# Reordering VectorE's routing work in a fused attention and mixture-of-experts kernel

## The reference: what is computed

```
A   = softmax(Q K^T / 4)
out = (0.6 * A + 0.4 * L) V          # L: a band of three neighbours on each side
x   = x + out Wo^T + bo
```

```
xn     = layernorm(x)
probs  = softmax(gelu(xn rW1 + rb1) rW2 + rb2)          # router, 512 hidden features
mask   = the two largest of four;  gate = probs * mask
x      = x + sum_e gate_e * (gelu((xn*mask_e) We1[e] + be1[e]) We2[e] + be2[e])   # 1024 hidden
```

## Time and profile before

| what | value |
|---|---|
| median of three runs | 2059.73 us (2054.78 to 2060.18) |
| profiled execution, its own time | 2075.05 us |
| its span | 2073.3 us |
| TensorE busy in the span | 2006.5 us (97%) |
| VectorE busy | 1647.4 us (79%) |
| ScalarE busy | 1403.4 us (68%) |
| GpSimd busy | 393.8 us (19%) |
| mean granted TensorE clock | 0.988 |
| attention and projection stages | about 0 to 1437 us of the span |
| routing | about 1437 to 1605 us |
| experts | from about 1605 us to the end |

### The profile page before, as it was taken

How to read it: one execution, slowest core, us unless ns; L and a number is a source line. 1 busy time by engine, 2 the same in 40 slices (tenths; PEclk the granted TensorE clock), 3 DMA queues, 4 the chain that set the end, 5 groups by cost and what they waited for, 6 DMA issues and landing times. The chain is left out here.

```text
span 2073.3 us, 48468 instructions
## 1 busy us (share of the span) xinstructions
PE 2006.5 (97%) x16588; PEld 1077.1 (52%) x16588; DVE 1647.4 (79%) x2007; ACT 1403.4 (68%) x2502; POOL 393.8 (19%) x461
## 2 busy tenths in 40 slices
PE   7999999999999999999999999998998899999997
PEld 4543333333333333333333333334876799999996
DVE  6788999999999999999999999970445555665564
ACT  3348888888888888888888888887554322222221
POOL 1360010010001000100100010010054433333333
PEclk9999999999999999999999999999999999999998
DMA  7934354335334533543453355320125567776671
GB/s 264 242 78 90 74 119 93 71 87 120 79 72 99 115 72 74 121 91 71 87 120 79 72 105 109 71 61 25 57 100 219 213 236 267 260 255 237 244 261 52
DMA packets 102092, 267.69 MB, mean 129 GB/s; under 512 B 22894, under 2 KB 45936, under 8 KB 95344
## 3 DMA queue, kind: packets, MB, share of 16 engines
q1 hardware_dynamic: 91648, 241.25, 44.0%
q0 software_dynamic: 10368, 25.45, 3.5%
HBM read 212.87 MB, written 74.20 MB: 138 GB/s over the span
## 5 line engine op out<-in xcount | busy, mean ns | idle before, releaser
L588 DVE TENSOR_REDUCE part_max<-psum_attend 128x1 f32<-128x1024 f32 x1024 | 1241.9, 1222 | 59.4 <-PE psum_attend L710 47.1
L643 ACT ACTIVATE probs<-psum_attend 128x512 f32<-128x512 f32 x2048 | 1111.1, 596 | 153.2 <-PE psum_attend L723 84.3
L723 PE MATMUL psum_attend<-score_q,score_k 50*128 50x512 f32 x2048 | 748.6, 448 | 2.9 <-DMA max_k<-qk_pieces 1.7
L710 PE MATMUL psum_attend<-max_k,max_q 48*128 48x512 f32 x2048 | 741.3, 451 | 0.8 <-DVE part_max L588 0.8
L735 PE MATMUL psum_attend<-probs,v_ones 128*32 128x256 f32 x8192 | 657.2, 393 | 9.4 <-ACT heads_sb L658 9.0
L723 PEld LDWEIGHTS psum_attend<-score_q,score_k 50*128 50x128 f32 x2048 | 308.3, 185 | 409.5 <-ACT probs L643 392.9
L735 PEld LDWEIGHTS psum_attend<-probs,v_ones 128*32 128x32 f32 x8192 | 162.4, 108 | 382.6 <-issue 200.8
L710 PEld LDWEIGHTS psum_attend<-max_k,max_q 48*128 48x128 f32 x2048 | 295.5, 186 | 13.8 <-issue 7.5
L1152 ACT ACTIVATE x_sb<-psum_route,x_sb 128x512 f32<-128x512 f32 x152 | 104.8, 690 | 285.7 <-PE psum_route L1513 248.9
L1532 PE MATMUL psum_route<-w,h_hi 128*128 128x256 f32 x1216 | 217.8, 278 | 0.0
L1532 PEld LDWEIGHTS psum_route<-w,h_hi 128*128 128x128 f32 x1216 | 195.9, 189 | 14.4 <-issue 1.1
(11 more groups left out here) (171 smaller groups left out, 1508.8 us busy)
## 6 DMA issues: line engine op xcount, KB each, us to landing
w<-w_split SPq DMA_DIRECT2D x38, 2048.0 KB
max_q<-qk_pieces SPq DMA_DIRECT2D x192, 128.0 KB, 7.4
score_k<-qk_pieces SPq DMA_DIRECT2D x192, 128.0 KB, 4.6
xs<-in_pads SPq DMA_DIRECT2D x33, 528.0 KB, 5.7
qk_pieces<-pieces SPq DMA_DIRECT2D x32, 512.0 KB, 4.8
w_split<-w_pair SPq DMA_DIRECT2D x32, 512.0 KB, 6.4
max_k<-qk_pieces SPq DMA_DIRECT2D x192, 64.0 KB, 7.5
score_q<-qk_pieces SPq DMA_DIRECT2D x192, 64.0 KB, 2.2
```

What stands on the lines that cost most here:

```text
L588: nc.vector.tensor_reduce(part_max[:, t, p:p + 1], ps_m[p].rearrange("q b f -> q (b f)"), axis=AXIS.X, op=ALU.max).then_inc(m_read, 1)
L643: nc.scalar.activation(probs[kb % 2][:, chunk * BLOCK:(chunk + 1) * BLOCK], bank_of(at), ACT.Exp, scale=float(HD) ** -0.5).then_inc(exp_do ...
L710: last = nc.tensor.matmul(ps_m[p][:, h, :], max_q[u][rows, t * P:(t + 1) * P], max_k[u][rows, p * BLOCK:(p + 1) * BLOCK], start=True, stop ...
L723: nc.tensor.matmul(bank_of(at), score_k[u][rows, kb * P:(kb + 1) * P], score_q[u][rows, part * BLOCK:(part + 1) * BLOCK], start=True, stop ...
```

## The change

VectorE's order in the routing loop changes; the instructions stay the same, and no other engine's program is touched. In round i, `normalise(i+1)` now follows the low parts at once. Then come `weigh(i-2)` and `give_slots(i-2)`, then `choose(i-1)`. The gates are thus made one round later than before (round i for block i-2). The first tile's `split_x(0)` and `prepare(0)` move behind the loop, and so behind `choose(6)`; `weigh(6)` and `give_slots(6)` follow them.

```diff
         for i in range(BLOCKS):
             dve.wait_ge(hi_ready, i + 1)
             nc.vector.tensor_tensor(xT_lo[:], ps_t, xT_hi[:].bitcast(F32), ALU.subtract).then_inc(lo_ready, 1)
-            if i >= 2:
-                give_slots(i - 2)
             if i + 1 < BLOCKS:
                 normalise(i + 1)
             else:
                 read_logits(i - 1)
-                split_x(0)
-                prepare(0)
+            if i >= 2:
+                weigh(i - 2)
+                give_slots(i - 2)
             if i >= 1:
                 choose(i - 1)
-                weigh(i - 1)
             if i == HALF + 1:
                 list_early()
+        split_x(0)
+        prepare(0)
+        weigh(BLOCKS - 2)
         give_slots(BLOCKS - 2)
```

## The result

The changed kernel takes 2088.84 us, the median of four runs (2086.94 to 2096.21), against 2057.36 for the one before on the same occasion (four runs, 2054.78 to 2060.18). The ratio is 1.0153, with a 95% interval of 1.0125 to 1.0181: 31.5 us more, 26 to 37 by the interval. The forecast was 2085, between 2074 and 2095; as a rise it was 24.9 us. The profiled execution took 2086.94 us (span 2085.1).

A forecast was written before the change was run, and what follows sets the result against it. TensorE, busy 2006.5 of 2073.3 us, was taken to bound the kernel. Delay 22.8 plus clock 9.8 less gains 5.1 and 2.6 gave +24.9 us on the 2059.7 median: 2085 us, range 2074 to 2095.

The forecast's parts named there:

- The mechanism: Rounds 2 to 5: heads wait for `place_read`, now given behind the next block's rows, 7.14 us after the projection.
- GpSimd's power: Power for block i+1 queues behind `scatter(i-3)` on GpSimd; claimed cost nought, with 10 us to spare.
- 22.8 us of delay: Heads of rounds 2 to 5 start 6.87, 5.69, 5.07 and 5.15 us later; the delays add up to 22.8 us.
- The clock's toll: Heads after each new idle time run partly at half clock: 2.45 us each, 9.8 in all, bounds nought to 18.0.
- The rival without the toll: The heads' wait is real but costs no clock: +15 us, 2075; chance 0.12.
- the one with the whole block at half clock: Heads all at half speed, or late signals: +33 to +36 us, 2093 to 2096; chance 0.12.
- The gains of rounds 6 and 7: No heads there; low parts and logits read come earlier: 5.1 us gained in round 6, 2.6 in round 7.
- The signals that come later than the modelled end: Lateness of the projection's own signal to VectorE: taken as nought; if all four came 2.23 late, 8.9 us more.
- the logits' 2.23 us: Round 3: ScalarE's copy of the logits came 2.23 us after the last thing it visibly needed.
- The faster rival: VectorE's 51.7 us of waits were what mattered and the heads don't stand: 2052 us; chance 0.04.

The follow-up runs named there:

- the second profile: The kernel before, profiled once more without any edit: it took 2054.5 us, with a routing stage of 155.82 us against 163.15 in its first profile.
- the second comparison: The changed kernel run once more, unedited, beside the kernel before: ratio 1.0168 (1.0137 to 1.0198), routing stage 188.22 us.
- ten instructions more: The changed kernel with ten more small VectorE instructions between gates and slots in rounds 2 to 5: median 2098.45 us, ratio to before 1.0172.

## Why the prediction was right

**The mechanism** stands. The forecast said that the heads would wait for `place_read` behind the next block's rows in rounds 2 to 5 only, by 7.14 us from the projection's end: 7.19 measured, 7.22 to 7.23 in the other three rounds. The closeness of that one number has some luck in it: from the sum to the first gate took 1501.58 - 1495.88 = 5.70 us instead of 5.91, and TensorE started 0.26 us after the end of the counts' read (1502.77), which the forecast did not have. Reading the counts alone ahead takes the four waits away, and adding to or taking from the chain moves them by as much. Everything else that the later slots could hold (scatters, buffers, GpSimd's power) cost nought, as forecast: with the counts alone read ahead, the rest of the profile is as long as with all slots ahead.

**The term "22.8 us of delay" was too small.** It was the step that took the idle times of rounds 3 to 5 as the kernel's own, with ScalarE's staging "in the shadow of the longer wait". They were of one execution. With heads that start right behind the projection, all four rounds lose what round 2 loses: 37.1 us by the second profile, less the clock's 9.0, is 28.1. The sign to heed was in the numbers at hand: the profiled execution was 15.3 us above the median, and part of that had to be somewhere.

**The clock's toll** was forecast at 9.8 us from the first heads block, 9.0 measured by filling the idle time. The nearest row was a good price. Most of the 0.8 is in the subtraction: 6.94 us runs to the modelled end of the block, 4.49 to the start of what follows. Taken to the same end, 1562.99 - 1558.36 = 4.63, it is 2.31 each, 9.2 in all. The rival without the toll falls, and so does the one with the whole block at half clock: from 1507.0 to 1509.7 us the granted clock was 0.89. (That rival's +33 to +36 has only +33.1, or +33.8 with the late signals, behind it in the forecast's terms.)

**The gains of rounds 6 and 7** were forecast at 5.1 and 2.6; 5.9 came in the stage, of which only some 4.4 belong to the order. Round 6 was read from that same execution: its second router group started 1584.70 - 1576.11 = 8.6 us after the projection, in the second profile 1575.15 - 1567.99 = 7.2, and after the change 1608.26 - 1604.76 = 3.5, as the forecast's 3.45 had it. So 3.7 us were to be had there, and the 1.43 us wait for the logits in round 7 did not exist in an undisturbed run. The forecast also left out that a short idle time can cost clock: by its rows, 1.0 to 1.6 us had not; here idle times of 2.49 and 2.57 us did in one profile and did not in another.

**The signals that come later than the modelled end** were set at nought for the projection; VectorE's sum started 0.04 us after it in the profile of after, so this holds. By the Trainium skill (Perfetto Trace Analysis, "Tensor Engine Instruction") the end is an estimate and the semaphore follows the acknowledged write; no run here shows a lateness that this alone would explain, since the late signals came in one profile of the kernel before and not in the other. So the logits' 2.23 us, which the forecast took as agreeing with that rule, were of that execution.

The two large errors went the same way: 5.3 too little for the delay and 3.3 too much for the gains, both of which make the sum too small. Against them stand 0.8 too much for the clock and 0.4 us ahead of projection 3. The sum was 24.9, the trace 32.4 (30.8 with the slow stretch of before in it), the times 31.5 and, in the second comparison, 34.6 (28 to 41). The forecast time was nearer than its sum by luck: it stood on a median of 2059.7 for before, and the one beside the changed kernel was 2.4 lower.

**The faster rival** had a true half. VectorE's wait for the exponentials did cost something, some 4.4 us in rounds 6 and 7. With all the slots ahead of the rows the kernel ends near where that rival put it, 4 to 12 us below before (its figure was 7.7).

## What to carry to other kernels

When an engine's steps are reordered, ask of each signal it gives, not of each wait it has, who stands behind it: here 44 of 51.7 us of waiting were removed from an engine with time to spare, and one signal, given by the second of five small instructions, came 7 us later for the engine without any. A step that both frees a buffer and does long work of its own should be cut, and the freeing part done first. And where one profiled execution lies above the median of the runs, take a second before its small idle times are used as terms of a sum.

## What was not expected of the hardware

An execution of the kernel before had TensorE's signals reach ScalarE and VectorE 1.6 to 8.7 us after the modelled end, with no cause in the profile. Its span is 20.6 us longer than that of the second profile (2073.3 for 2052.7): 3.0 ahead of the first heads, 7.3 in the routing stage, 9.8 in the first expert tile. No other profile of this study has such signals.

The granted clock does not follow from the order of the instructions alone. After idle times of 2.49 and 2.57 us in round 6 it fell to 0.50 for 3.3 us in one profile and stayed at 1.00 in another with the same idle times; where such a stretch fell, it moved 1.6 us from one stage of the profile to the next. How long the clock stays low differs too: behind the four waits of 8.8 us of "ten instructions more" the same heads block took 6.57, 7.34, 6.12 and 7.11 us, for 6.68 to 6.80 behind the 6.8 us of after. What decides it, no run here tests.

And filler work pays: 27 matmuls whose result is thrown away, 6.4 us each time in a wait of 6.8, took 9.0 us off the stage, and brought the kernel from 1.53% to 0.88% above before, since the useful matmuls behind them then ran at the full 2.4 GHz.
